# Local attention over eight sequences: the keys' and queries' finishing product runs one step on, and GpSimd splits inputs and weights in place of VectorE

## The reference

```
x = attn_layer(shift_tokens(x), Wqkv[i], q_scale[i], k_scale[i], Wo[i]) + x
x = ffn_layer(shift_tokens(x), ln_g[i], ln_b[i], W1[i], b1[i], W2[i], b2[i]) + x

attn_layer:  q, k, v = split(x @ Wqkv)              # 16 heads of 64
             q = l2norm(q) * q_scale;  k = l2norm(k) * k_scale
             q, k = rotary(q) * scale, rotary(k) / scale
             windows of 32 queries see 64 keys; softmax; @ v; @ Wo
ffn_layer:   layer norm; a, gate = split(xn @ W1 + b1); (a * gelu(gate)) @ W2 + b2
```

## Time and profile before

| | |
|---|---|
| median of 3 runs | 5493.87 us (5483.84 to 5496.69) |
| profiled execution, its own time | 5499.49 us |
| its span | 5497.7 us |
| TensorE busy | 4684.0 us, 85% of the span |
| VectorE busy | 3694.6 us, 67% |
| ScalarE busy | 3155.3 us, 57% |
| GpSimd busy | 2034.8 us, 37% |
| row maxima of the six layers | 1901.2 us to 5427.3 us in the span |

### The profile page before, as it was taken

The page is one execution under the profiler, slowest core; times in us unless marked ns, Lnnn a source line. Parts: engine busy times, 40 slices in busy tenths (PEclk is TensorE's granted clock), DMA queues, the critical chain, the costliest instruction groups (busy, mean ns, idle before and its releaser), DMA issues. The chain is left out here.

```text
span 5497.7 us, 160430 instructions
## 1 busy us (share of the span) xinstructions
PE 4684.0 (85%) x63808; PEld 2744.8 (50%) x63808; DVE 3694.6 (67%) x5172; ACT 3155.3 (57%) x9549; POOL 2034.8 (37%) x1438
## 2 busy tenths in 40 slices
PE   7888888777777689989999899988998899999986
PEld 3333333322222356556666566655665566566553
DVE  5666677533333477777777777777777777777773
ACT  4444444323232367766776677666776766666774
POOL 2222222200000255554555455544555455545551
PEclk9999999877777799999999999999999999999997
DMA  1000000000000333344333433334333433343332
GB/s 45 0 0 0 0 0 0 24 0 0 0 0 0 98 87 87 84 97 94 86 86 91 97 85 87 85 92 96 86 88 93 98 84 87 90 97 86 85 85 74
DMA packets 197282, 340.10 MB, mean 62 GB/s; under 512 B 63568, under 2 KB 63568, under 8 KB 195024
## 3 DMA queue, kind: packets, MB, share of 16 engines
q1 hardware_dynamic: 196560, 330.14, 25.5%
HBM read 34.19 MB, written 6.29 MB: 7 GB/s over the span
## 5 line engine op out<-in xcount | busy, mean ns | idle before, releaser
L377 ACT ACTIVATE c_Pb<-c_S,c_nb 128x64 f32<-128x64 f32 x3072 | 918.0, 325 | 853.6 <-DVE c_nb L663 853.0
L342 POOL TENSOR_TENSOR c_F<-c_tAB 128x1024 f32<-128x1024 f32 x384 | 906.9, 2362 | 367.3 <-DMA c_QK<-c_F 213.8
L330 POOL TENSOR_TENSOR c_Pb<-c_Pb,c_rs 128x512 f32<-128x512 f32 x384 | 400.4, 1043 | 1426.0 <-DVE c_rs L671 1426.0
L644 DVE SCALAR_TENSOR_TENSOR c_tAB<-c_PA,c_WP,c_base 128x1024 f32<-128x1024 f32 x384 | 492.2, 1282 | 306.2 <-PE c_PA L450 305.9
L377 ACT ACTIVATION_READ_ACCUMULATOR c_Pb<-c_S,c_nb 128x1 f32 x3072 | 666.3, 217 | 0.0
L644 DVE SCALAR_TENSOR_TENSOR c_tAB<-c_PB,c_WP,c_base 128x1024 f32<-128x1024 f32 x384 | 491.6, 1280 | 58.8 <-PE c_PB L450 57.1
L334 POOL TENSOR_TENSOR c_sq<-c_sq 128x512 f32<-128x512 f32 x384 | 501.6, 1306 | 3.3 <-issue 2.4
L525 PE MATMUL c_S<-c_PTs,c_VE 64*64 64x32 f32 x10752 | 430.6, 222 | 62.3 <-DVE c_PTs L677 28.9
L659 DVE COPY c_VO<-c_PB 128x512 f32<-128x512 f32 x384 | 263.9, 687 | 320.4 <-PE c_PB L485 320.1
L651 DVE SCALAR_TENSOR_TENSOR c_F<-c_PD,c_F 128x1024 f32<-128x1024 f32 x384 | 466.6, 1215 | 9.0 <-ACT c_PD L368 8.8
L525 PE MATMUL c_S<-c_PTs,c_VO 64*64 64x32 f32 x13824 | 442.9, 222 | 22.8 <-issue 22.1
(11 more groups left out here) (247 smaller groups left out, 9597.9 us busy)
## 6 DMA issues: line engine op xcount, KB each, us to landing
c_QK<-c_F SPq DMA_DIRECT2D x3072, 64.0 KB, 2.0
c_VE<-c_VO SPq DMA_DIRECT2D x384, 128.0 KB
c_VE<-c_VO SPq DMA_DIRECT2D x384, 96.0 KB
c_stage<-in_w_heads SPq DMA_DIRECT2D x24, 256.0 KB, 2.9
c_WT<-in_w_tails SPq DMA_DIRECT2D x6, 1024.0 KB, 6.7
a_W<-in_w_level SPq DMA_DIRECT2D x1, 3335.5 KB, 10.7
c_WT<-in_w_tails SPq DMA_DIRECT2D x6, 537.5 KB, 4.3
b_W<-in_w_level SPq DMA_DIRECT2D x1, 3133.0 KB, 10.2
```

Of the source, the lines that this page charges most:

```text
L330: nc.gpsimd.tensor_tensor(p, p, rs[:, n % 2, :].unsqueeze(2).broadcast_to([P, HS, KEYS]), ALU.mult).then_inc(*p_ready.up())
L342: nc.gpsimd.tensor_tensor(F[:, j % 2], tAB[:, j % 2, 0], tAB[:, j % 2, 1], ALU.add).then_inc(*rotated.up())
L377: e = nc.scalar.activation(Pb[:, n % 2, i, :], S[:, n % 2, r, c * KEYS:(c + 1) * KEYS], ACT.Exp, bias=nb[:, n % 2, r * PS + c:r * PS + c + ...
L644: nc.vector.scalar_tensor_tensor(out=tAB[:, kind, half], in0=bank[:, :].unsqueeze(1).broadcast_to([P, 2, SEQ]), scalar=WP[:, 2 * kind + ha ...
```

## The change

On SyncE and VectorE, `permute` and `finish` take the job that is four steps back in place of three (`job_finished`). VectorE runs `finish` right behind `row_max`, ahead of `residual`, `scale`, `hidden(1)` and `v_copy`, where it ran behind the second `products`. SyncE issues `permute` ahead of `shift_values`, where it was behind it. `rotate`, `scores` and `sumsq` wait for the same jobs as before. `shift` and `divide` move to GpSimd, with a no-operation ahead of the copy, behind `add_squares` and ahead of `normalise`: `shift` in step 0, `divide` in steps 1, 2, 4 and 6. `take_scales` gets a wait for VectorE's own earlier products.

```diff
--- before.py
+++ after.py
@@ -203,6 +203,9 @@
         def job_before(n, now, nxt):
             return (n - 3) % NS, nxt if n >= 3 else now
 
+        def job_finished(n, now, nxt):
+            return (n - 4) % NS, nxt if n >= 4 else now
+
         def v_unit(n, now, nxt):
             return (n + 3) % NS, nxt if n >= 5 else now
 
@@ -282,12 +285,12 @@
                     sp.dma_start(WT[:, lo:hi], w[:, lo:hi]).then_inc(done.sem, 16)
 
                 def step(n, now, nxt, prev, new, fresh):
-                    jb, tb = job_before(n, now, nxt)
+                    jf, tf = job_finished(n, now, nxt)
                     v, tv = v_unit(n, now, nxt)
+                    if tf:
+                        permute(jf, tf)
                     if v % 2 and tv:
                         shift_values(v // 4, v % 4 // 2, tv)
-                    if tb:
-                        permute(jb, tb)
                     if new is not None:
                         if n == 0:
                             load_scales(new)
@@ -324,6 +327,25 @@
             def _(pool):
                 nc.gpsimd.memset(x1s[:, 0:1], 0.0).then_inc(*zeroed.up())
 
+                def shift(turn, now):
+                    if now and not now.first:
+                        pool.wait_ge(*layer_done.nth(-2, now))
+                    src, x = xf[:, turn.seq * (SEQ + 1):turn.seq * (SEQ + 1) + SEQ], turn.seq % 2
+                    pool.nop(nofuse=True)
+                    nc.gpsimd.tensor_copy(xh[:, x], src).then_inc(*shifted.up())
+                    pool.wait_ge(*shifted.nth(1, turn))
+                    nc.gpsimd.tensor_tensor(xl[:, x], src, xh[:, x].bitcast(F32), ALU.subtract).then_inc(*shifted.up())
+
+                def divide(k, layer):
+
+                    pool.wait_ge(wh_in[k % 2].sem, layer * 32 + 16 * (k // 2 + 1))
+                    c, w = H_QK + 512 * k, stage[:, k % 2]
+                    hi, lo = WH[:, c:c + 512], WL[:, c:c + 512]
+                    pool.nop(nofuse=True)
+                    nc.gpsimd.tensor_copy(hi, w).then_inc(*split.up())
+                    pool.wait_ge(*split.nth(2 * k + 1, Turn(layer, 0, 1)))
+                    nc.gpsimd.tensor_tensor(lo, w, hi.bitcast(F32), ALU.subtract).then_inc(*split.up())
+
                 def normalise(n, turn):
                     pool.wait_ge(*rs_ready.nth(n + 1, turn))
                     p = Pb[:, n % 2]
@@ -346,11 +368,20 @@
                     jb, tb = job_before(n, now, nxt)
                     if tb:
                         add_squares(jb, tb)
+                    if nxt and now and n == 0:
+                        shift(nxt, now)
+                    if new is not None:
+                        for at, k in ((1, 0), (2, 1), (4, 2), (6, 3)):
+                            if n == at:
+                                divide(k, new)
                     if now:
                         normalise(n, now)
                     if tj:
                         rotate(j, tj)
 
+                shift(Turn(0, 0, seqs), None)
+                for k in range(PIECES):
+                    divide(k, 0)
                 turns(pool, step)
 
             @block.scalar
@@ -623,14 +654,6 @@
 
             @block.vector
             def _(dve):
-                def shift(turn, now):
-                    if now and not now.first:
-                        dve.wait_ge(*layer_done.nth(-2, now))
-                    src, x = xf[:, turn.seq * (SEQ + 1):turn.seq * (SEQ + 1) + SEQ], turn.seq % 2
-                    nc.vector.tensor_copy(xh[:, x], src).then_inc(*shifted.up())
-                    dve.wait_ge(*shifted.nth(1, turn))
-                    nc.vector.tensor_tensor(xl[:, x], src, xh[:, x].bitcast(F32), ALU.subtract).then_inc(*shifted.up())
-
                 def products(j, half, turn):
                     kind = j % 2
                     bank, table = (PB, base[:, kind, 0:2]) if half else (PA, base[:, kind, 1:3])
@@ -710,28 +733,23 @@
                         nc.vector.scalar_tensor_tensor(out=xf[rows, at + skew:at + skew + SEQ], in0=PC[rows, :], scalar=par("b2")[rows, :],
                                                        in1=x1s[rows, skew:skew + SEQ], op0=ALU.add, op1=ALU.add).then_inc(*layer_done.up())
 
-                def take_scales(layer):
+                def take_scales(layer, now=None):
+                    if now:
+                        dve.wait_ge(*prods.nth(2 * JOBS, now))
 
                     dve.wait_ge(wp_in.sem, layer * 16 + 16)
                     nc.vector.tensor_copy(WP[:, :], WN[:, :]).then_inc(*scales.up())
 
-                def divide(k, layer):
-
-                    dve.wait_ge(wh_in[k % 2].sem, layer * 32 + 16 * (k // 2 + 1))
-                    c, w = H_QK + 512 * k, stage[:, k % 2]
-                    hi, lo = WH[:, c:c + 512], WL[:, c:c + 512]
-                    nc.vector.tensor_copy(hi, w).then_inc(*split.up())
-                    dve.wait_ge(*split.nth(2 * k + 1, Turn(layer, 0, 1)))
-                    nc.vector.tensor_tensor(lo, w, hi.bitcast(F32), ALU.subtract).then_inc(*split.up())
-
                 def step(n, now, nxt, prev, new, fresh):
                     j, tj = job(n, now, nxt)
-                    jb, tb = job_before(n, now, nxt)
+                    jf, tf = job_finished(n, now, nxt)
                     v, tv = v_unit(n, now, nxt)
                     if new is not None and n == 2:
-                        take_scales(new)
+                        take_scales(new, now)
                     if now:
                         row_max(n, now)
+                    if tf:
+                        finish(jf, tf)
                     if prev and n == 2:
                         residual(prev)
                     if prev and n == 4:
@@ -750,25 +768,14 @@
                         hidden(2, prev)
                     if tj:
                         products(j, 1, tj)
-                    if tb:
-                        finish(jb, tb)
                     if now:
                         pt_copy(n, now)
                     if prev and n == 7:
                         finish_turn(prev)
-                    if nxt and now and n == 0:
-                        shift(nxt, now)
-                    if new is not None:
-                        for at, k in ((1, 0), (2, 1), (4, 2), (6, 3)):
-                            if n == at:
-                                divide(k, new)
 
                 for i in range(2):
                     nc.vector.memset(nb[:, i, :], 0.0).then_inc(*layer_done.prime())
                 dve.wait_ge(*zeroed.nth(1))
-                shift(Turn(0, 0, seqs), None)
-                for k in range(PIECES):
-                    divide(k, 0)
                 dve.wait_ge(base_in.sem, 16)
                 take_scales(0)
                 turns(dve, step)
```

## The result

The changed kernel takes 5631.86 us (median of 4 runs, 5626.76 to 5644.69) beside 5490.15 us for the kernel before: a ratio of 1.0262, with a 95% interval of 1.024 to 1.0284. It is 142 us slower. I had forecast 196 us, with a range that holds the result.

The account below looks back on a forecast made before the run. TensorE was taken as the bound, busy 3247.6 of the layers' 3640 us. 42 turns at +4.5, five at +1.4 and the last at 0 gave +196 us: median 5690 us, own range 5627 to 5753, widened to 5590 to 5765.

Parts of the forecast that it names:

- Part 1: Sequence split leaves VectorE for GpSimd: gain 0.0 in steps 0 and 1; GpSimd's 2.5 us pair hidden in 5.7 us.
- Part 2: Finishing product one step on, 2.33 us later: an ordinary turn 4.5 us longer, bounds 3.0 and 6.0 us.
- (b): Step 2: finish pushes residual and value copy, for which TensorE's second projection waits: +0.5 us.
- (a): Step 3: job 7's later product releases transfers and so scores later, step 10.3 to 10.6 us: +2.0 us.
- (c): Steps 4 to 6: later permutes delay `rotate`, the squares' addition and TensorE's `sumsq`: +1.5 us.
- (d): Step 7: `hidden(1)` pushed 1.2 us back, TensorE's value product waits for it: +0.5 us.
- (e): Steps 0 and 1: value copy pushed 0.9 us and permutes later, covered by waits and TensorE's work: 0.0.
- Part 3: New weights' splits on GpSimd: five turns gain 3.1 us against the 4.5, so +1.4 us each.
- my signs: Signs of being right included step 3 at 10.3 us or more and TensorE's share in the layers about 85%.
- Only the scores' wait costs: Rival: (b), (c) and (d) are absorbed; +79 us, 5573 us; chance 0.10.
- VectorE's relief pays: Rival: step 1's row maximum starts 2.43 us earlier and TensorE follows; 149 us gain, 5345 us; chance 0.05.
- GpSimd becomes the bound: Rival: dearer pair and later `rotate` make `normalise` late in step 0, 1 to 2 us a turn; 5762 us; chance 0.12.

Follow-up runs that it names:

- e1: Kernel before, with only the two kinds of splits (`shift`, `divide`) moved to GpSimd and the new wait in `take_scales`: 5500.70 us, ratio 1.0009.
- e7: Changed kernel with two more subtractions of 512 columns on GpSimd in step 0, ahead of the copy in `shift`: 5641.98 us, ratio 1.0288.
- e6: Changed kernel, but job 7 alone finished and permuted in step 2, as before: 5558.60 us, ratio 1.0128.
- e5: Changed kernel, but with the finish behind the value copy: 6178.63 us, ratio 1.1231.
- e10: e6 with `hidden(1)` ahead of the finish in step 7: 5527.37 us, ratio 1.0083 to the kernel before.
- e3: Kernel before, with only SyncE's `permute` put ahead of `shift_values`: 5460.82 us, ratio 0.9963.
- e2: Changed kernel with `shift` and `divide` back on VectorE, so only finish and permute are one step on: 5707.32 us, ratio 1.0396.
- e8: e1 with the scales and first two pieces of new weights loaded at the head of step 0: 5450.19 us, ratio 0.9934.

## Why the prediction was right, and which sizes were off

**Part 1, right.** The split's removal from VectorE brings nothing, because TensorE is full in steps 0 and 1: 17.73 us beside 17.74, and e1 at 1.0009. GpSimd's pair costs 0.61 + 1.28 us in the row of e7, against my 2.5 us with its wait. The room of 5.7 us held even two subtractions more.

**Part 2, right in direction in every term, with two sizes too large, one path wrong and one cost missing.**

| term | forecast | by medians | by means | tested by |
|---|---|---|---|---|
| (b) step 2 | +0.5 | +0.57 | +0.66 | the trace alone |
| (a) step 3 | +2.0 | +1.28 | +1.31 | e6: 1.6 a turn, with the clock |
| (c) steps 4 to 6 | +1.5 | +0.59 | +0.93 | e5: the loop, not its size |
| (d) step 7 | +0.5 | +0.47 | +0.43 | e10: 0.5 a turn |
| (e) steps 0 and 1 | 0.0 | -0.01 | +0.21 | the trace alone |
| turn | +4.5 | +2.9 | +3.5 | |

In (a) and (c) the mis-sized step is the same: the time from the start of the finish to the release by its transfers, which I put at 8.4 us.

In (a) I had read 8.84 us off one turn and taken 0.44 us off it for the wait behind the values' shift. The median over 36 turns is 9.20 us before, and 8.12 us after. In the step shown above it is 7.87 us, and SyncE waited for nothing but the finish: its last issue of the shift ended at 3383.37, the finish at 3384.03, and the first permuting issue began at 3384.05. So the release moved from 7.47 to 8.73 us behind the row maximum, by 1.26 us, and step 3 grew by 1.28. e3, which has the new order on SyncE alone, has 8.51 us: 0.69 us of the gain is the order, which I had at 0.44, and the other 0.4 us came with the finish's new place.

In (c) the transfers of job 0 release `rotate` of step 4, and there the time is 7.76 us in place of 8.4. In the turn shown, `sumsq` of step 5 starts 11.91 us behind the row maximum of step 4 (3391.89), against 11.3 before and 12.7 forecast:

```profile
3403.80 1.12 PE L503 MATMUL c_PD<-c_sq,c 128*128 128x512 f32 x2 [0.33 <-POOL c_sq L356]
```

It does wait for GpSimd's addition, as (c) says, but it is only 0.6 us late and not 1.4. Step 4 grew for another reason, the one that stands in (b) too.

That reason is the wrong path. In (b) I had TensorE's transposes wait for the value copy, by way of the second projection and the centring product. The second projection did move as forecast, to 3.9 us behind the row maximum in the turn shown. But the transposes wait for something else:

```profile
3379.13 0.19 DVE L694 RECIPROCAL c_rs<-c_sums 128x8 f32<-128x8 f32 x1
...
3379.40 1.04 POOL L352 TENSOR_TENSOR c_Pb<-c_Pb,c_rs 128x512 f32<-128x512 f32 x1 [2.18 <-DVE c_rs L694]
...
3380.50 0.66 PE L541 MATMUL c_S<-c,c_Pb 128*128 128x128 f32 x4 [0.54 <-POOL c_Pb L352]
```

The finish also pushes VectorE's reciprocals, from 4.32 to 5.10 us behind the row maximum of step 2 in the median. GpSimd's `normalise` waits for them, and TensorE's transposes for `normalise`: in 36 of 36 ordinary turns before, where the earlier trace rows already shows a wait of 0.20 us, and in 25 of 36 after. In step 4 the reciprocals moved from 4.38 to 4.71 us, and the step grew 0.42 us. Both paths of step 2 moved by about the same (0.63 and 0.78 us), so that the forecast of +0.5 us came out near is partly luck. No run separates them.

The missing cost is TensorE's clock in step 4, which no term of mine has. It takes 0.9 us in ten of 36 turns and 1.8 us in seven. e6 shows that it belongs to the wait of (a).

A relief that I had left out goes the other way: the second operation of the scale in step 4 (L697 before, L720 after) takes 0.54 us in the mean and not 1.15. These are the rows of the group view, the first from the kernel before and the second from the changed one:

```profile
L697 DVE TENSOR_SCALAR c_xn<-c_xn,c_WT 128x512 f32<-128x512 f32 x48 | 55.3, 1153 | 1.7
```

```profile
L720 DVE TENSOR_SCALAR c_xn<-c_xn,c_WT 128x512 f32<-128x512 f32 x48 | 26.0, 542 | 1.7
```

This is the blocking that the Trainium skill describes in "SBUF — State Buffer", section on who interferes with whom, and the trace agrees. In the kernel before, 46 of the 48 ran beside GpSimd's addition of the squares, and took 1.18 us; in the changed one 43 of 48 ran beside nothing of GpSimd's, and took 0.49 us. It comes with the place of the finish and not with the splits, as e1 still has 1.20 us and e2 has 0.49. How much of the 0.6 us reaches the turn isn't shown.

**The rule on transfers.** The Trainium skill's "DMA: Bandwidth & Descriptors", section on rules for kernel authors, says to issue early and wait late. By it alone step 3 would have grown by 2.33 us; it grew by 1.28. The direction is right. The size needs what the rule doesn't look at, the order and the pace of the issues ahead of the landing.

**Part 3, right in direction, with sizes off.** I forecast +1.4 us for a turn with new weights and the trace shows +0.5 (79.35 us beside 78.83). Their extra over an ordinary turn fell from 6.8 to 4.4 us, a gain of 2.4 us where I had 3.1; but the 4.5 us that I set against it was 2.9. My 2 us for the wait on the first piece was near: GpSimd idles 2.3 to 2.9 us there in step 1 of the changed kernel, and the step is 1.6 us longer than in an ordinary turn. Step 2 is 0.2 us longer, and steps 3 and 4 are 1.4 and 1.5 us longer, where I had 0.7 us for step 2 and 1.1 us for SyncE's extra issues; I haven't separated what holds them. In e1, where the permute comes later, the same wait is 7.4 to 8.2 us, and in e8 without it these turns cost nothing extra.

**The sum.** By the medians of the steps, 42 x 2.9 + 5 x 0.5 = 124 us of the measured 142. By whole turns nothing is missing: 42 turns grew by 3.4 us in the mean, five by 0.6, and the last, which I had put at 0, by 3.3 (2.3 of them in its step 3), 149 us from the first row maximum to the last but for rounding. The first row maximum came 3.7 us earlier, where I had said ±3 us and taken 0, and the profiled executions differ by 145 us.

That the result lies in the range owes something to luck. By the medians the turn's +2.9 us is just under my lower bound of 3.0, and (a) is under its own of 1.5; the clock, which I didn't foresee, brings it to 3.5. The two bounds of the range also carry the five turns at +1.4 us unchanged, though their gain is set against the same 3.0 or 6.0; done in step, the lower bound would be 5619 us in place of 5627. Two of my signs did not come: step 3 is at 9.96 us and not at 10.3 or more, and TensorE's share in the layers is 87% (3300.0 of 3785 us from 1840 on) and not 85%.

**The rivals.** "Only the scores' wait costs" is refuted by e6, which keeps 1.3% after nearly all of that wait is gone, and by e10. "VectorE's relief pays" is refuted by e1. "GpSimd becomes the bound" is refuted by e7 in step 0.

## What to carry to other kernels

Moving an operation to where its own engine has a hole also moves everything that it releases. Before doing so, follow its result through the transfers to the next consumer, and look whether that consumer waits already: here the scores and `rotate` did. An engine with time to spare is only cheap for work whose inputs are there: GpSimd takes the splits for nothing, but a wait for a late load at the head of its queue costs more than the splits, and with an earlier load the same splits come with a gain of 0.7%. Look at the granted clock of the step behind a wait, too: here the wait of step 3 cost its own 1.3 us and, in 17 of 36 turns, 0.9 or 1.8 us more in step 4. And add up whole turns beside the medians of steps, or such a cost goes unseen.

## What the runs showed of the hardware that I hadn't expected

TensorE's granted clock fell behind a wait, and the next step paid for it. In the two turns of the changed kernel shown above, TensorE idles 2.4 and 2.6 us in step 3, 1.55 and 2.08 us of them right before the scores of step 4, and in 17 of 36 turns the mean clock of step 4 is 0.84 or less. With most of that wait gone (e6) it is 1.00 in all 36. At full clock step 4 takes 7.89 us in both. What decides in which turns it falls stays open.

VectorE's split of 512 columns costs 1.08 + 1.64 us beside a working GpSimd and 0.43 + 0.69 us alone. In e2 the split stays on VectorE, but 43 of its 48 copies in step 0 no longer meet an operation of GpSimd's and take 0.42 us, and step 0 is at 8.93 us in place of 10.72. Most of the relief of step 0 came without moving the split, by the later finish alone.

SyncE's issues have two lengths. Of the 3072 permuting issues, most take 0.59 us (the median in each trace), but in the kernel before 442 took over 0.8 us, up to 2.15, and in the changed kernel only 140. e1 has 443 and e3 428, e2 132 and e5 145, so it goes with the place of the finish in the step and not with GpSimd or the order on SyncE. Eight issues in a row took 5.2 us from first to last start in the median before and 4.4 us after; for job 7 it was 5.24 us before, 5.13 in e3 and 4.57 after, which is most of what the finish's new place brought in (a). In the kernel before, about half of the long issues (52%) began beside TensorE's value projection, against 9% of the others. After the change it is 13% and 11%, so that isn't the cause by itself. What lengthens an issue stays open: no run here was made to tell it.
